# Identity products that nothing reads, on TensorE between its stages: a two-layer transformer kernel on one NeuronCore

## The reference

```python
x = _layernorm(x + _L0_attn_ref(x, ...))   # 16 heads of 16, softmax(q k^T / 4) v, then Wo
x = _layernorm(x + _L0_ffn_ref(x, ...))    # 8 experts, best 2 of each token, 256 -> 1024 -> 256, gelu
x = _layernorm(x + _L1_attn_ref(x, ...))   # two wavelet levels along the sequence, linear attention, synthesis
x = _layernorm(x + _L1_ffn_ref(x, ...))    # 8 experts, best 2, 256 -> 256 -> 256, silu, an expert over its
                                           # capacity of 1280 tokens is dropped
```

## Time and profile before

| what | us |
|---|---|
| median of 3 runs | 1918.9 (1912.54 to 1919.27) |
| the profiled execution, its own time | 1918.68 |
| its span in the trace | 1916.9 |
| TensorE busy in it | 1693.4 (88%) |
| VectorE busy | 1136.4 (59%) |
| ScalarE busy | 900.9 (47%) |
| TensorE's mean granted clock | 0.943 |

### The profile page before, as it was taken

The page is one execution under the profiler, slowest core; times in us unless marked ns, Lnnn a source line. Parts: engine busy times, 40 slices in busy tenths (PEclk is TensorE's granted clock), DMA queues, the critical chain, the costliest instruction groups (busy, mean ns, idle before and its releaser), DMA issues. The chain is left out here.

```text
span 1916.9 us, 38693 instructions
## 1 busy us (share of the span) xinstructions
PE 1693.4 (88%) x11908; PEld 1095.9 (57%) x11909; DVE 1136.4 (59%) x2420; ACT 900.9 (47%) x1539; POOL 395.1 (21%) x559
## 2 busy tenths in 40 slices
PE   8999999999999999998489999999999389934771
PEld 4524434344444444437379999999999357924551
DVE  4688898989898989857821111111111487877224
ACT  4436777776776777772023333333333252230233
POOL 2310000000000100040023333333333100001771
PEclk9969999999999999998799999999999699977886
DMA  6501221222112221325735656565656300034545
GB/s 208 187 20 48 59 60 56 57 58 56 56 56 59 58 59 55 114 72 169 275 104 174 185 170 187 168 189 167 188 164 176 107 1 1 1 132 136 69 53 175
DMA packets 118379, 207.52 MB, mean 108 GB/s; under 512 B 22065, under 2 KB 88177, under 8 KB 108849
## 3 DMA queue, kind: packets, MB, share of 16 engines
q1 hardware_dynamic: 89280, 171.29, 28.0%
q0 software_dynamic: 20352, 22.92, 7.5%
q10 hardware_dynamic: 8688, 12.58, 1.9%
HBM read 163.65 MB, written 56.10 MB: 115 GB/s over the span
## 5 line engine op out<-in xcount | busy, mean ns | idle before, releaser
L607 DVE TENSOR_REDUCE unit_max<-ps_ring 128x1 f32<-128x512 f32 x1024 | 640.3, 683 | 78.5 <-PE ps_ring L500 72.3
L593 ACT ACTIVATE w<-ps_scores 128x1024 f32<-128x1024 f32 x512 | 498.1, 1022 | 239.2 <-PE ps_scores L562 239.2
L500 PE MATMUL ps_ring<-k_stack,q_stack 96*128 96x512 bf16 x1024 | 360.1, 393 | 10.6 <-POOL v_padded L458 7.9
L562 PE MATMUL ps_scores<-q_stack,k_stack 98*128 98x512 bf16 x1024 | 307.4, 382 | 2.6 <-ACT w L593 2.5
L1498 PEld LDWEIGHTS m_ps_h<-m_xt,w1s 128*128 128x128 f32 x2272 | 266.7, 193 | 4.5 <-issue 0.9
L1498 PE MATMUL m_ps_h<-m_xt,w1s 128*128 128x128 f32 x2272 | 267.2, 276 | 0.6 <-issue 0.6
L1508 PE MATMUL m_ps_y<-w,m_ht 128*128 x1136 | 261.0, 383 | 0.0
L522 PE MATMUL ps_o<-w,v_padded 128*32 128x256 f32 x4096 | 260.6, 383 | 0.0
L500 PEld LDWEIGHTS ps_ring<-k_stack,q_stack 96*128 96x128 bf16 x1024 | 98.7, 97 | 253.8 <-DVE unit_max L607 180.5
L1508 PEld LDWEIGHTS m_ps_y<-w,m_ht 128*128 128x128 f32 x1136 | 210.1, 190 | 29.7
L1530 ACT ACTIVATE m_ht<-m_ps_h,w1s 128x128 f32<-128x128 f32 x568 | 162.4, 368 | 96.6 <-PE m_ps_h L1498 96.6
(11 more groups left out here) (260 smaller groups left out, 1544.8 us busy)
## 6 DMA issues: line engine op xcount, KB each, us to landing
w1s<-in_w SPq DMA_DIRECT2D x71, 1028.0 KB
o_raw<-o_transposed SPq DMA_DIRECT2D x64, 128.0 KB
rows<-g_rows SPq DMA_DIRECT2D x16, 512.0 KB, 5.3
y<-sums SPq DMA_DIRECT2D x16, 512.0 KB, 7.6
q_parts<-qk_part SPq DMA_DIRECT2D x16, 384.0 KB, 2.8
k_parts<-qk_part SPq DMA_DIRECT2D x16, 384.0 KB, 2.8
q_stack<-q_parts SPq DMA_DIRECT2D x64, 96.0 KB
k_stack<-k_parts SPq DMA_DIRECT2D x64, 96.0 KB
```

The costliest lines, as they stand in the source:

```text
L500: nc.tensor.matmul(out[:, :], qs[0:STACK, u, qt * P:(qt + 1) * P], ks[0:STACK, u, half * HALF:(half + 1) * HALF], start=True, stop=True).t ...
L562: mm = nc.tensor.matmul(p_s[kt % 2][:, half * HALF:(half + 1) * HALF], ks[:, u, kt * P:(kt + 1) * P], qs[:, u, half * HALF:(half + 1) * HALF],
L593: nc.scalar.activation(pt[:, kt, :], p_s[kt % 2][:, :], ACT.Exp, scale=SCALE)\
L607: nc.vector.tensor_reduce(unit_max[:, u % 2, half, qt:qt + 1], src[:, :], axis=AX.X, op=ALU.max).then_inc(ring_used, count)
```

## The change

A helper multiplies an identity by itself, `count` times, into a PSUM bank that nothing reads. It is called at eleven places, all on TensorE (the one in the gate runs once for each layer, the one among the maxima 32 times): 141 products in all. Three of the calls come with a wait of their own, at the end of the projection, in the channels and at the end of the wavelet stage.

```diff
+def keep_awake(nc, ident, out, count, cols):
+    blocks = cols // P
+    for _ in range(count):
+        nc.tensor.matmul(out[:, 0:cols].rearrange("p (n r) -> p n r", r=P), ident[:, :],
+                         bcast(ident[:, :].unsqueeze(1), [P, blocks, P]), start=True, stop=True)
 # stage_project, TensorE
+                keep_awake(nc, c.ident, pq[3], 20, P)
                 for b in range(B):
                     products(b)
+                pe.wait_ge(part1_ready, B * 8 - 3)
+                keep_awake(nc, c.identb, pq[0], 15, HALF)
 # stage_attention, TensorE
+                keep_awake(nc, c.identb, p_s[0], 14, HALF)
                 pe.wait_ge(init, 5)
                 for at, u, qt, half in first_units():
...
                     max_unit(u, qt, half, at, ring[at % RING])
+                    keep_awake(nc, c.identb, p_s[0], 1, HALF)
...
                 pv(NH - 1, SLOTS - 1, BURSTS - 1)
+                keep_awake(nc, c.identb, p_s[0], 3, HALF)
 # stage_output, TensorE
+                keep_awake(nc, c.ident, p_idle, 8, 2 * P)
                 pe.wait_ge(c.wo_loaded, 16)
                 for i in range(NT // 2):
...
+                keep_awake(nc, c.ident, p_idle, 9, HALF)
 # stage_gate, TensorE (both layers)
+                keep_awake(nc, c.ident, p_g, 4, 2 * P)
                 turn(0)
 # stage_experts_tiles, TensorE
+                keep_awake(nc, c.ident, p_y[1], 12, HALF)
                 turn_x(0, 0, 0)
 # stage_channels, TensorE
+                pe.wait_ge(loaded[HALVES - 2], 16)
+                keep_awake(nc, c.ident, p_tr[3], 6, HALF)
                 for b in range(B):
 # stage_wavelet, TensorE, behind the last tile
+                pe.wait_ge(norm_ready, 2 * B)
+                keep_awake(nc, c.ident, banks[0], 14, HALF)
```

More of the change, by code:

```diff
@@ L686, in stage_output @@
         p_y = [mem.ps(f"c_ps_y{u}") for u in range(4)]
+        p_idle = mem.ps("c_ps_idle")
         made, summed = mem.sem("c_made"), mem.sem("c_summed")
```

## The result

The changed kernel takes 1927.0 us (median of 6 runs, 1925.55 to 1928.58) against 1917.3 for the kernel before (6 runs, 1912.54 to 1920.6): a ratio of 1.0047 with a 95% interval of 1.0035 to 1.006. The forecast was 1927 with a range of 1915 to 1935. The profiled execution took 1925.55 us with a span of 1923.7, against 1918.68 and 1916.9. The sum of +8.2 us can be tested term by term in these two traces, which are 6.9 us apart; the medians are 9.8 us apart. Of all runs in this document one, of the fitted version with the gates' products put back (1939.17 us at a granted clock of 0.912), was in a slower state, and its median leaves it out.

The account below looks back on a forecast made before the run. Added products were taken to win back only half of TensorE's work at 1.2 GHz where it sets the pace, and to delay stages where they outlast pauses. Terms summed to +8.2 us on 1918.7, so 1927, range 1915 to 1935.

Parts of the forecast that it names:

- Start, +0.4: Before the projection: 20 products run to 9.4 us, then full clock as if begun at 9.1 before; +0.4 us.
- Projection's end, +1.6: End of the projection: 15 products run to 94.9 us, past VectorE's 93.55, and the block's end waits for TensorE; +1.6 us.
- Attention, -3.5: Attention's prologue and first head: full clock wins 1.8 us in the head, 2.0 before it, less 0.3; -3.5 us.
- Rival (b): Attention's prologue stays at half clock, slower still, and the first head wins nothing: +20 us, 1939; chance 0.08.
- Output projection, +4.3: Output projection: 8 products delay it 3.4 us, full clock shortens it, 9 more make the block end with TensorE; +4.3 us.
- Gate 0, -1.7; gate 1, -0.3: Gates: 4 products start the transposes 0.6 us late, full clock wins 2.3 and 1.0; -1.7 and -0.3 us.
- First experts, +3.3: First experts: 12 products take 10.3 us, first tile done at 982.4 against 979.2, nothing gives it back; +3.3 us.
- Channels, 0: Channels: added records end around when TensorE is wanted; VectorE sets the stage and TensorE catches up; 0 us.
- Wavelet's end, +4.1: End of the wavelet stage: 28 records take 14.6 us, to 1704.2, after VectorE's end at 1699.94; +4.1 us.
- Rival (c): Clock falls in the pauses that remain and rises late in channels, experts or output: up to +6 us, 1933; chance 0.14.
- Rival (d): Whole kernel: nothing measurable, since pauses elsewhere (stores, loads of weights) take up the delays: 1919; chance 0.05.
- rival (e): Gates: transposes don't hold the clock, so the gates win nothing and lose 0.6 us twice: +3, 1930; chance 0.02.

Follow-up runs that it names:

- the fitted version: Changed kernel with counts fitted to the pauses (none at the start, ahead of the output projection or at the gates) against the kernel before: 1912.6 us, ratio 0.9976.

## Why the prediction was right, and where its terms were not

- **Start, +0.4.** Measured -0.15. The first product was 2.4 us late as worked out, and the clock rose 4.5 us after TensorE began instead of 5.1. Right, and within the scatter of this place. (The bound for a rise at the very end was added up wrongly: 40 records of 0.23 us end at 11.4, which is +2.3 and not +1.5.)
- **Projection's end, +1.6.** Measured +1.51 against the last product of v, +1.36 at the first maximum itself. Right, and with it the choice that a block's end waits for TensorE's array; that is what most of the sum hung on. The term's own two ends, 94.9 and 93.55, are 1.35 apart.
- **Attention, -3.5.** Measured -2.43. The steady half was right (first head 12.2 instead of 13.4 us), but I had the first head come down to 11.56, and it did not: in the fitted version, where the clock stayed up, it takes 133.88 - 121.65 = 12.2 too. So 0.6 us of the first head isn't the clock's. 0.5 us more went with 3.4 us of half clock, which began 1.3 us into the prologue; I had taken 0.3 for it. A clock of 0.50 in the prologue was one of my signs of being wrong; it came for these 3.4 us of 19. Rival (b), the prologue at half clock for good, fell.
- **Output projection, +4.3.** Measured +4.66 up to the gate's block. Size and mechanism right; the eight products in front, which I took as the price of full clock, weren't needed for it.
- **Gate 0, -1.7; gate 1, -0.3.** Measured +0.09 and -0.52. The step that failed: I costed TensorE's transposes and took their gain to the block's end. They did win it (6.47 to 3.66 us, and TensorE's last product ends 2.1 us earlier after the block opens), but the end did not move with TensorE: the block's stores, which begin with its first rows, are done after it. The windows of before show TensorE's end and the stores' within 2 us of each other, and I had not looked at who is next. The stage takes 26.4 to 27.8 us in the ten traces, from its opening to the route's first product, and before and after (27.7 both) lie at the upper end, so +0.09 is good to about 1 us only.
- **First experts, +3.3.** Measured +0.92. The first tile is as forecast: 5.38 us late at its start, 1.96 us of it won back by the second tile, +3.4. The other 70 tiles gave back 2.5 us more, where I wrote that nothing would. I don't take it for an effect of the change: from the second tile to the last it takes 507.3 us here and between 507.9 and 510.0 in the nine other traces, 509.8 in that of before, with no order by what stands ahead of it. A single pair of traces reads this stage only within 2.7 us.
- **Channels, 0.** Measured 0. The call did nothing: it put the first transpose 0.6 us later, and VectorE, which sets the stage, took that up.
- **Wavelet's end, +4.1.** Measured +4.52. The products ran to 1709.3; 15.0 us instead of 14.6, and 0.4 is the difference.
- **The bounds.** Their terms add up to +4.3 and +14.4, where +4.5 and +15 were written; this changes nothing.
- **Second experts, not in the sum.** Measured -1.73 from the second route on; from the experts' first transpose to the end it is 148.3 before and 146.5 after. No call stands there. The ten traces give 146.5 to 149.4, the fitted version the highest. I can't tell a cause from scatter, and it stays open.

The terms that were too hopeful (gate 0 by 1.8, attention by 1.1) and those too dark (experts by 2.4, second experts by 1.7) nearly cancel. The median comes out on the forecast to 0.1 us by more luck than the terms deserve: in the profiled executions the difference is 6.9 us where 8.2 was the sum, in the medians 9.8. Rival (c) came true in one place, the 3.4 us of half clock in the prologue, at 0.5 us instead of 6. Rival (d), no measurable effect because pauses take the delays up, was right at gate 0 for a gain, and for a delay only in the channels, with 0.6 us.

On the clock and transposes, the fitted version shows the same again as the earlier trace rows: it fell at 894.9, and rose at 898.3 with only transposes on TensorE since 895.51:

```profile
894.90:898.30 3.40, 2.79 (x13) 2.79 (x14) 3.40 (x11) 2.74 (x6) 0.43 (x1) 0.50 0.05 6
898.30:900.40 2.10, 2.10 (x21) 2.03 (x19) 1.60 (x5) 2.03 (x5) 0.00 (x0) 1.00 1.01 338
```

The Trainium skill, page "TensorE: Matmul & The Clock Gate", Part 4, has it that full clock doesn't engage for transposes. This kernel's traces disagree, and rival (e), which the page would bring, fell: the gates' transposes ran at full clock.

## What to carry to other kernels

Unread work on an engine is free only while nothing of the program is ready for that engine, and at a barrier only while another engine is still at work: size each piece by the wait that it fills, read from the trace, and cut it when it ends later than the engine beside it. Keeping TensorE's clock up was worth 5 us in 1917 here once fitted. 3.2 us of it came at the start of attention, where short products fill the pause and stand behind each real one while TensorE is half idle ahead of a stage that it paces. Three in a pause of 2 us gave TensorE 1.7 us more, of which between nothing and 1.4 us reached the block's end. Before counting such a gain at the end of a stage, ask which engine or store finishes second.

## What the runs showed of the hardware that I had not expected

- Three bfloat16 products (0.82 us by their record) in a pause of 2 us went with a clock of 1.00 into the output projection in all nine changed versions; in the trace of the kernel before, without them, it was at half for 3.5 us. No run took away these three alone.
- TensorE busy 97% by its records at half clock did not raise the clock in 30.7 us, the first 18 at VectorE's pace, the last 12 with products 0.43 us apart. In the other stages read here it rose 2.8 to 5.7 us after TensorE's first work. With an unread product behind each it was at 1.00 throughout, or again 3.4 to 6.8 us after it had fallen.
- Behind the same pause ahead of attention the clock fell in the changed kernel (at 102.4) and in the version with the three longest calls cut, and not in the run with 24 products ahead of the experts; the code of the three is the same up to there. It cost 0.5 us.
